# Counting edges by destination: running counts from ScalarE's Sign in place of one-hots from VectorE

## The reference

```python
deg = segment_sum(ones, dst + loops)        # in-degree of each node, plus 1 for its own loop
dinv = rsqrt(deg)
norm = dinv[src] * dinv[dst]
h = segment_sum((x @ W)[src] * norm[:, None], dst + loops) + b
```

## Time and profile before

| what | value |
|---|---|
| timed runs, median (3) | 5606.13 us (5601.16 to 5618.05) |
| profiled execution: span from first to last instruction, its only time on record | 5967.4 us |
| mean granted TensorE clock over the span | 0.792 |
| busy over the span: VectorE, TensorE, GpSimd, ScalarE | 64%, 59%, 51%, 39% |
| counting phase in the trace | 21 to 187 us |

### The profile page before, as it was taken

One profiled execution on the slowest core, in us unless ns is written; L12 is line 12 of the kernel. 1 busy time (PEld: TensorE's weight loads), 2 busy tenths in 40 slices (PEclk: granted clock), 3 DMA queues, 4 the chain that ended last, 5 costly groups with the idle time before them and its releaser, 6 DMA issues. The chain is left out here.

```text
span 5967.4 us, 70027 instructions
## 1 busy us (share of the span) xinstructions
PE 3527.0 (59%) x19808; PEld 2717.4 (46%) x19808; DVE 3844.7 (64%) x11203; ACT 2300.9 (39%) x5320; POOL 3031.0 (51%) x2733
## 2 busy tenths in 40 slices
PE   5677766267712466631455644444799993775443
PEld 1344445267611255531355542333577772664443
DVE  9666568379835466621465566666678882666998
ACT  0233330068810255521122222333466662334776
POOL 8666557625567422376655516776155555552000
PEclk9898887689955688965677776766899996997666
DMA  4455559479857777621455427777356653775554
GB/s 181 125 150 153 151 146 331 143 227 310 273 163 265 254 244 248 229 84 55 122 188 194 149 52 212 241 245 226 143 204 212 211 209 99 235 244 196 208 209 160
DMA packets 698336, 1147.11 MB, mean 192 GB/s; under 512 B 110368, under 2 KB 453459, under 8 KB 691702
## 3 DMA queue, kind: packets, MB, share of 16 engines
q1 hardware_dynamic: 594752, 959.48, 48.6%
q0 software_dynamic: 103200, 183.16, 10.5%
HBM read 689.93 MB, written 464.79 MB: 194 GB/s over the span
## 5 line engine op out<-in xcount | busy, mean ns | idle before, releaser
L2378 POOL DMA_INDIRECT sc_rows<-layer,node_idx x400 | 385.1, 963 | 264.3 <-DVE sc_xin L2393 135.6
L2252 PE MATMUL ro_end<-vals,end_mask 128*2 128x128 f32 x1600 | 243.0, 317 | 388.4 <-DVE vals L2116 243.2
L778 PE MATMUL msg_acc<-msg_pair,msg_vals 128*128 128x512 f32 (+3 forms) x400 | 210.2, 699 | 310.8 <-issue 147.5
L2903 POOL DMA_INDIRECT tf_edge_x<-y,tf_src_idx x200 | 198.0, 990 | 382.9 <-SPq L2879 334.2
L208 POOL DMA_INDIRECT x_src<-in_x_dram,node_idx x200 | 329.7, 1649 | 81.6 <-issue 60.7
L3049 PE MATMUL tf_o_ps<-pre_w,tf_hidden 128*128 128x128 f32 (+1 forms) x3136 | 362.2, 276 | 5.8 <-issue 5.2
L2252 PEld LDWEIGHTS ro_end<-vals,end_mask 128*2 128x2 f32 x1600 | 148.3, 96 | 474.0 <-DVE vals L2116 252.0
L3037 PE MATMUL tf_h_ps<-tf_x_t,pre_w 128*128 128x512 f32 x784 | 350.2, 600 | 19.1 <-ACT tf_hidden L2997 18.0
L3049 PEld LDWEIGHTS tf_o_ps<-pre_w,tf_hidden 128*128 128x128 f32 (+1 forms) x3136 | 356.6, 192 | 7.7 <-issue 7.6
L2278 PE MATMUL ro_acc<-vals,ro_mask 128*126 128x128 f32 x1600 | 240.4, 314 | 201.6 <-ACT ro_square L2210 87.0
L1611 POOL DMA_INDIRECT cap_own<-layer,w_own x200 | 204.5, 1022 | 292.2 <-SPq L1591 242.1
(11 more groups left out here) (487 smaller groups left out, 11220.1 us busy)
## 6 DMA issues: line engine op xcount, KB each, us to landing
ro_mask<-masks SPq DMA_DIRECT2D x100, 504.0 KB
layer<-zeros SPq DMA_DIRECT2D x96, 512.0 KB
si_both<-layer SPq DMA_DIRECT2D x48, 1024.0 KB
ro_far<-far SPq DMA_DIRECT2D x75, 512.0 KB
ro_both<-both SPq DMA_DIRECT2D x75, 512.0 KB
agg<-zeros SPq DMA_DIRECT2D x48, 512.0 KB
mom_x<-in_x_dram SPq DMA_DIRECT2D x48, 512.0 KB
mom_agg<-agg SPq DMA_DIRECT2D x48, 512.0 KB
```

Of the source, the lines that this page charges most:

```text
L778: mm = nc.tensor.matmul(acc[g % 3][:, i:GT, :].rearrange("p t e -> p (t e)"), vals[:, u, i, :], pair[:, u, FIRST[i]:FIRST[i] + GT - i, :]. ...
L2252: mm = nc.tensor.matmul(end_ps[0:2, j, :], k.end_mask[:, t, :], k.vals[:, t, :], start=True, stop=True, skip_group_check=True)
L2378: nc.gpsimd.indirect_dma_start(out=rows[:, g % SC, c * GT + j, :], out_offset=None, in_=k.layer1, in_offset=bass.IndirectOffsetOnAxis(ap=k ...
```

## The change

Of the two high one-hots of a step, VectorE keeps the one for `src`. For `dst` ScalarE makes a step function in its place: Sign(column - high + 0.5), which is -1 in columns below the edge's high part and +1 from it on. The matmul with the low one-hot then adds, for each low part and column, the number of edges whose high part is at most the column, minus the number of those above: twice the running count less the row's total. At the end VectorE copies this table out of PSUM, subtracts from each column its left neighbour (for column 0 it adds the last column, which holds the row's total), and scales by 0.5 and adds 1 for the degree. The bias 0.5 - high of all steps is made by one VectorE instruction ahead of the loop. ScalarE waits for that, and in each step, from the fifth on, for `used`. TensorE waits for the one-hot before the first matmul of a step and for the step function before the second. Two semaphores are added (`stepped`, `offset`), and the phase clears nine in place of seven.

```diff
--- before.py
+++ after.py
@@ -215,7 +215,10 @@
     nc = k.nc
     with ExitStack() as st:
         hot_low = k.sb(st, "cnt_hot_low", [P, 2, 2, GT, P], FP16)
-        hot_high = k.sb(st, "cnt_hot_high", [P, 4, 2, NCOL], FP16)
+        hot_high = k.sb(st, "cnt_hot_high", [P, 4, NCOL], FP16)
+        step_high = k.sb(st, "cnt_step_high", [P, 4, NCOL], FP16)
+        half_less = k.sb(st, "cnt_half_less", [P, T])
+        twice = k.sb(st, "cnt_twice", [P, NCOL])
         scan = k.sb(st, "cnt_scan", [P, NCOL])
         count = k.sb(st, "cnt_count", [P, NCOL])
         root = k.sb(st, "cnt_root", [P, NCOL])
@@ -226,6 +229,8 @@
         whole = k.sb(st, "cnt_whole", [P, NCOL])
         low_made = k.sem(st, "cnt_low_made")
         hot = k.sem(st, "cnt_hot")
+        stepped = k.sem(st, "cnt_stepped")
+        offset = k.sem(st, "cnt_offset")
         used = k.sem(st, "cnt_used")
         step = k.sem(st, "cnt_step")
         based = k.sem(st, "cnt_based")
@@ -257,10 +262,11 @@
                 def highs(n):
                     if n >= 4:
                         dve.wait_ge(used, n - 3)
-                    for a in range(2):
-                        nc.vector.tensor_scalar(hot_high[:, n % 4, a, :], k.iota_high16[:, :],
-                                                k.high_col[:, a, n:n + 1], None, ALU.is_equal).then_inc(hot, 1)
-
+                    nc.vector.tensor_scalar(hot_high[:, n % 4, :], k.iota_high16[:, :],
+                                            k.high_col[:, 0, n:n + 1], None, ALU.is_equal).then_inc(hot, 1)
+
+                nc.vector.tensor_scalar(half_less[:, :], k.high_col[:, 1, :], -1.0, 0.5, ALU.mult,
+                                        ALU.add).then_inc(offset, 1)
                 for g in range(EG):
                     lows(g)
                     for n in range(g * GT, (g + 1) * GT):
@@ -268,7 +274,13 @@
                 nc.vector.memset(one_col[:, :], 1.0).then_inc(step, 1)
                 dve.wait_ge(used, T)
                 nc.vector.tensor_copy(count[:, :], table[0][:, 0:NCOL]).then_inc(step, 1)
-                nc.vector.tensor_scalar(k.degree[:, :], table[1][:, 0:NCOL], 1.0, None, ALU.add).then_inc(step, 1)
+                nc.vector.tensor_copy(twice[:, :], table[1][:, 0:NCOL]).then_inc(offset, 1)
+                dve.wait_ge(offset, 2)
+                nc.vector.tensor_tensor(k.degree[:, 1:NCOL], twice[:, 1:NCOL], twice[:, 0:NCOL - 1], ALU.subtract)
+                nc.vector.tensor_tensor(k.degree[:, 0:1], twice[:, 0:1], twice[:, NCOL - 1:NCOL],
+                                        ALU.add).then_inc(offset, 1)
+                dve.wait_ge(offset, 3)
+                nc.vector.tensor_scalar(k.degree[:, :], k.degree[:, :], 0.5, 1.0, ALU.mult, ALU.add).then_inc(step, 1)
                 dve.wait_ge(step, 3)
 
                 dve.wait_ge(based, 1)
@@ -287,6 +299,12 @@
 
             @block.scalar
             def _(act):
+                act.wait_ge(offset, 1)
+                for n in range(T):
+                    if n >= 4:
+                        act.wait_ge(used, n - 3)
+                    nc.scalar.activation(step_high[:, n % 4, :], k.iota_high16[:, :], ACT.Sign,
+                                         bias=half_less[:, n:n + 1]).then_inc(stepped, 1)
                 act.wait_ge(step, 3)
                 nc.scalar.activation(root[:, :], k.degree[:, :], ACT.Sqrt).then_inc(rooted, 1)
 
@@ -300,16 +318,17 @@
                     g = n // GT
                     if n % GT == 0:
                         pe.wait_ge(low_made, 2 * g + 2)
-                    pe.wait_ge(hot, 2 * n + 2)
-                    for a in range(2):
-                        mm = nc.tensor.matmul(table[a][:, 0:NCOL], hot_low[:, g % 2, a, n % GT, :], hot_high[:, n % 4, a, :],
-                                              start=False, stop=False, skip_group_check=True)
-                    mm.then_inc(used, 1)
+                    pe.wait_ge(hot, n + 1)
+                    nc.tensor.matmul(table[0][:, 0:NCOL], hot_low[:, g % 2, 0, n % GT, :], hot_high[:, n % 4, :],
+                                     start=False, stop=False, skip_group_check=True)
+                    pe.wait_ge(stepped, n + 1)
+                    nc.tensor.matmul(table[1][:, 0:NCOL], hot_low[:, g % 2, 1, n % GT, :], step_high[:, n % 4, :],
+                                     start=False, stop=False, skip_group_check=True).then_inc(used, 1)
 
                 pe.wait_ge(step, 2)
                 nc.tensor.matmul(base[:, 0:NCOL], k.before[:, :], count[:, :], start=True, stop=True)
                 nc.tensor.matmul(total[:, 0:NCOL], k.ones[:, :], count[:, :], start=True, stop=True).then_inc(based, 1)
-        clear_semaphores(nc, [low_made, hot, used, step, based, rooted, filled])
+        clear_semaphores(nc, [low_made, hot, stepped, offset, used, step, based, rooted, filled])
 
 
 def paced(eng, k, sem, value):
```

## The result

The changed kernel takes 5563.3 us (median of four runs, 5553.35 to 5576.53) against 5610.6 us for the kernel before in the same series: ratio 0.9913, 95% interval [0.9895, 0.9931], which is 39 to 59 us less. A second series of five runs gave 5567.79 against 5615.58, ratio 0.9915 [0.9900, 0.9929]. The medians are 47.3 and 47.8 us apart; 45.2 were forecast. The timed runs bear out a gain of this size, and the trace of the phase says what it consists of.

The account below looks back on a forecast made before the run. VectorE was taken to set the counting phase's pace. 46.2 - 0.2 - 0.5 - 0.2 - 0.15 = 45.2 us saved, median 5606.1 to 5561 us (chance 0.74, own range 5550 to 5572); overall range 5545 to 5590.

Parts of the forecast that it names:

- (1): VectorE's counting loop: one high one-hot per step removed, 4 x 0.231 us per group, 46.2 us saved over 50 groups.
- (2): ScalarE in the loop: 200 Signs added at 0.51 us, 2.04 per group, hidden beside VectorE's 2.13 by 0.09 us.
- rival B: Counting loop: ScalarE becomes the bound at 0.62 us per Sign, 124 us in all, 27.7 saved, 5578 us; chance 0.09.
- (3): Loop hand-offs between ScalarE, VectorE and TensorE: new waits cost 0 per group, bounds 0 and 0.31 us.
- (4): Start of the counting phase: 0.2 us for the half_less instruction and 0.5 us once for TensorE's first eight matmuls.
- (5): Tail of the counting phase: new copy, subtraction and scaling about 0.2 us late, two more semaphore clears 0.15 us.
- (6): Rest of the program behind the barrier: cost 0, plus or minus 8 us.
- C: Counting loop: TensorE at its lower clock, 2.64 us per group, 132 us, 20.7 - 1.0 saved, 5586 us; chance 0.05.
- D: End of the counting phase: GpSimd's long gather, tied to the clock, holds it; only 7.3 us go, 5599 us; chance 0.06.
- One sign that the prediction named: In the new profile, GpSimd's long gather was to end near 130 us, following the count copy.
- E: Counting loop: buffer ring locks step, producers and TensorE take turns, 0.955 us per step, 191 us, 5645 us; chance 0.04.
- the milder form of rival D: GpSimd's gathers advance once per VectorE group; each left over costs 1.24 us behind the loop, with room for five more.

Follow-up runs that it names:

- e3: Changed kernel with VectorE making low one-hots for src alone, read by both matmuls (dst counts then wrong): 5562.33 us.
- e10: Changed kernel with only the low one-hots laid out part by step, so both compare inputs run in unit steps: 5567.43 us.
- e7: Changed kernel with two buffers instead of four each for the high one-hot and the step function: 5592.84 us in one run.
- e6: Changed kernel with one buffer instead of four each for the high one-hot and the step function: 5728.15 us, ratio 1.0200.
- e12: Changed kernel again, no edit, for a second profile and more timed runs: 5567.79 us, ratio 0.9915.
- e4: Changed kernel with Sign and its matmul over the first 196 columns only (half the dst counts left out, degree 1): 5569.03 us, ratio 0.9925.
- e5: Changed kernel with low one-hots for src alone and Sign and its matmul over 196 columns (dst counts wrong, degree 1): 5534.88 us, ratio 0.9854.
- e2: Changed kernel with the step functions made on VectorE (compare, then minus 0.5) in place of ScalarE's Sign: 5612.78 us, ratio 1.0004.
- e8: Kernel before with a second operation (times 1.0) in its high one-hots: 5622.75 us in one run.
- e11: Kernel before with its high one-hots in two tensors instead of one: 5609.52 us in one run.
- e9: Changed kernel with low one-hots laid out part by step and every fourth step's dst one-hot back on VectorE: 5556.96 us, ratio 0.9909.

## Why the prediction was right

- **The engine that sets the pace, and the price of what goes (1).** 4 x 0.231 us per group was the right row: the period fell from 3.06 to 2.13, 50 times, 46.2 us.
- **Sign at 0.51 us (2).** e3 shows 0.511. The margin of 0.09 us per group was real and small: e3 and e10 run at 2.04. The length of one Sign is 0.61 us; whoever takes this as its price gets rival B. The Trainium skill (ScalarE: Activation LUTs, What ACT_TABLE_LOAD costs) states the overlap of about 93 ns that the rule I had weighed leaves out, and 280 ns + 0.833 ns per element with a pointer bias: by an estimate from these figures 0.607 us for one and 0.514 from start to start. The trace agrees with both (0.61 and 0.511).
- **Hand-overs at nothing (3).** Right with four buffers; e7 and e6 show the price with two (2.77 us per group) and one (1.25 us per step).
- **Start (4).** Sized at 0.7, measured 1.1, and a further 0.5 stood in no term. The first group took 24.20 - 21.82 = 2.38 us and the second 27.13 - 24.20 = 2.93, 1.05 more than two periods of 2.13; the kernel before lost 0.13 in its first group (24.86 - 21.67 = 3.19), so 0.92 net, with 0.18 for half_less ahead of them. The price mis-sized is that of TensorE's slow start. Its first six matmuls of the loop come 0.33 us apart and last 0.50 to 0.54 us, as at the lower clock in e6, though the granted clock on record is 1.00 there too, and VectorE waits for them in the second group. The further 0.5: four of the groups that begin between 29 and 45 us take 2.24 to 2.26 us, as their four highs last 1.12 to 1.13 us in place of 1.00. GpSimd's gathers run until 45.13; behind that no group is so long, and e12 shows the same four (2.24 to 2.25). In e4, with slower gathers, none is. That the gathers are the cause was not tested. VectorE in order of time, the kernel before:

```profile
21.67 1.29 DVE L253 TENSOR_TENSOR cnt_hot_low<-iota_row,low_col 128x512 f16<-128x512 f16 x2 [0.88 <-PEq L70]
...
24.86 1.28 DVE L253 TENSOR_TENSOR cnt_hot_low<-iota_row,low_col 128x512 f16<-128x512 f16 x2
```

The changed kernel:

```profile
21.64 0.27 DVE L268 TENSOR_SCALAR cnt_half_less<-high_col 128x200 f32<-128x200 f32 x1 [0.88 <-PEq L70]
21.82 1.31 DVE L258 TENSOR_TENSOR cnt_hot_low<-iota_row,low_col 128x512 f16<-128x512 f16 x2
...
24.20 1.28 DVE L258 TENSOR_TENSOR cnt_hot_low<-iota_row,low_col 128x512 f16<-128x512 f16 x2
...
27.13 1.29 DVE L258 TENSOR_TENSOR cnt_hot_low<-iota_row,low_col 128x512 f16<-128x512 f16 x2
...
29.25 1.29 DVE L258 TENSOR_TENSOR cnt_hot_low<-iota_row,low_col 128x512 f16<-128x512 f16 x2
30.46 1.13 DVE L265 TENSOR_SCALAR cnt_hot_high<-iota_high,high_col 128x392 f16<-128x392 f16 x4
31.51 1.28 DVE L258 TENSOR_TENSOR cnt_hot_low<-iota_row,low_col 128x512 f16<-128x512 f16 x2
```

- **Tail (5).** 0.2 forecast, 0.0 measured, as the idle time took up all of it; behind the loop VectorE waits 0.37 us longer for TensorE (0.56 against 0.19), which was in no term. The clears: 142.69 - 140.94 = 1.75 us against 1.68, so 0.07 instead of 0.15.
- **The sum.** 46.2 - 1.1 - 0.5 - 0.4 - 0.1 = 44.1 with the measured terms; 45.2 forecast, 44.3 and 44.4 in the two profiles. Part of the agreement is luck: the start was 0.4 too cheap and two terms of 0.5 and 0.4 were missing, while tail and clears were 0.3 too dear. Against the main term of 46.2 all of this is small. The 3 us by which the timed gain exceeds the stage's are within the scatter of the rest of the program (6), and the forecast of the whole is no better than that.
- **The rivals.** B is excluded by e3 and e4. C is excluded by the granted clock (1.00 from 30 to 130 us, 0.97 over the phase) and by TensorE's matmuls 0.165 us apart; the clock does fall to 0.50 when the ring is cut to one buffer (e6). D is excluded: the last gather ends at 45.13, long before VectorE. One sign that the prediction named did not come, though: the long gather was to end near 130, with VectorE's loop, and there was none. That reading of the gather failed; no term of the sum rests on it. E was rightly described and is what one buffer gives: 5728 where it said 5645, as TensorE's lower clock and the lows between the steps were not counted.

The gathers of the changed kernel, against the earlier trace rows:

```profile
36.68 1.30 POOL L208 DMA_INDIRECT x_src<-in_x_dram,node_idx  x1 [0.30 <-issue]
...
44.19 0.94 POOL L208 DMA_INDIRECT x_src<-in_x_dram,node_idx  x1 [0.30 <-issue]
```

## What to carry to other kernels

Price an instruction that is added to a queue by the distance between starts, not by its length, and put it together from rows that share its width and its kind of operands. When work is moved to an idle engine, the gain ends where that engine fills up: here VectorE at 2.13 and ScalarE at 2.04 us per group came out nearly level, so that a further edit to either alone was worth about 4 us at most and to both 30. Small waits hide in a trace when neighbouring instructions overlap; two engines without idle time need not both be the limit.

## What the hardware showed beside this

- **GpSimd's gathers can fall into step with VectorE's groups.** In the kernel before they take 2.75 us, in e4 1.82 and in e5 1.22, each 0.30 us behind the last, so one starts every 3.05, 2.13 and 1.53 us: once in each group of VectorE, as the milder form of rival D had it. That a gather takes 0.94 us and VectorE's row of highs on top fits the first two (0.94 + 1.85 and 0.94 + 0.92), but not e5, where the row is again 0.92 us long. In the changed kernel (0.94 to 1.37 us), e7 and e10 they are not in step. The Trainium skill (GPSIMD Engine Reference, Specifications) names SBUF interfaces shared with VectorE, with contention in its two-port modes or with two SBUF inputs. That the gathers' pace hangs on VectorE's groups fits this; no run here shows in which mode the one-hots run. And in e2 VectorE works at the same pace as before without a gap, with compares and two-operation compares in turn, and the gathers take 0.94 to 1.43 us. Neither the second operation (e8) nor the place of the outputs (e11) is what frees them. What does is open. The gathers of e5:

```profile
43.87 1.23 POOL L208 DMA_INDIRECT x_src<-in_x_dram,node_idx  x1 [0.30 <-issue]
45.40 1.23 POOL L208 DMA_INDIRECT x_src<-in_x_dram,node_idx  x1 [0.30 <-issue]
```

- **One gather of 116.5 us** stood in both profiles of the kernel before and one of 122.6 in e8, each to about the end of VectorE's loop; in e11, with the same instructions, there was none. Its cause is open. It was not on the path: the last gather of the kernel before ends 7.3 us ahead of VectorE, and e2 without it takes as long.
- **A compare of two fp16 inputs, 128x512,** takes 0.335 us where both run in unit steps (e9, e10) and 0.60 where one repeats a single element. The Trainium skill (VectorE: DVE Perf Modes, the section on Mode 2×_1P) gives two results per cycle for that case; the trace agrees as far as the time falls by nearly half. The weights that it makes, then read by TensorE in steps of eight bytes, load in 0.11 us instead of 0.10.
